# Passage between two stages, end of the kernel and a wait of GpSimd laid out anew

## The chip, the cores and the metric

One core of a Trainium2 chip runs the kernel. Its engines are TensorE (PE), VectorE (DVE), ScalarE (ACT), GpSimd (POOL) and SyncE (SP, which only issues transfers here); each runs its own queue of instructions in order, and they meet at semaphores. The metric is device time in microseconds of one launch, the median of the runs.

## The reference

A cross attention and a gated feed-forward layer, each added to its input, over x of 128 x 64 x 128 (batch, sequence, channels) in fp32, with 16 heads of 8 channels:

```python
x = x + attention(layernorm(x), ctx, ctx)      # per batch 64 x 64 scores, 16 heads
z = layernorm(x)                               # 8192 rows of 128
def gate(z, conv_w, conv_b, gamma, beta, lin_w, lin_b):
    xc = einsum('ngf,gf->ng', z.reshape(n, 32, 4), conv_w) + conv_b
    xn = batchnorm(xc)                         # mean and variance over ALL 8192 rows
    return softmax(gelu(xn) @ lin_w.T + lin_b) # 128 logits per row
so, si = gate(z, so_...), gate(z, si_...)      # keep the 32 largest of 128 in each row
out_branch = (z @ W) * top32(so)
in_branch  = (z * top32(si)) @ W
x = x + out_branch + in_branch + bias
```

The batch norm needs every row before the first gate can be computed. That splits the kernel in two.

## The kernel before

The 128 batches are worked on in 16 groups of 8 (4 "pairs" of 128 rows, 512 tokens). **The first stage** is a software pipeline over steps t = -3 to 18. For a group: ACT normalises x, TensorE projects queries and keys, both are split into three bf16 parts (`split_keys`, L897, and `split_queries`, L910, on POOL; DVE does the queries of groups 0 and 1), SP writes the parts to DRAM and reads them back stacked (`write_parts` L247, `stack` L261), so that a single bf16 product has nearly fp32 accuracy. `query_side` (L348) computes the scores by row, DVE takes their maxima (`row_max` L733) and parts them into two bf16 numbers (`max_parts` L741: a CAST at L744, a subtraction at L746), TensorE turns these, ACT copies them (`max_out` L578) and sends them into the stack; `key_side` computes the scores by column with the maximum already subtracted, ACT takes the exponential, `values` multiplies, `normalise` and `residual` finish x. Then DVE takes row statistics (`stats` L722), POOL works out the scale and shift of the layer norm (`rstd` L878: add, pow, product, product), ACT normalises (L550), TensorE turns and convolves (`turn_x2`, `convolve`), ACT stores the 64 gate channels of the group (L631) and DVE takes their statistics (L802).

On POOL the order of a step t is: `rstd(t+3)` of the attention's norm, `split_keys(t+2)`, `split_queries(t+2)`, `rstd(t-2)` of the second norm, `add_bias(t+1)`. On SP: loads of ctx (t+3) and x (t+5), stack of keys and then of queries of group t+1 (12 transfers), writes of the parts of group t+2.

**The passage**: when group 15's gate channels are in, DVE aggregates (L840), POOL makes the batch norm's scale and shift in five small instructions (L941 to L949), ACT, which meanwhile has renormalised groups 0 and 1 (`again`, L648: 8 activations), loads the Gelu table with an activation on nothing (L659) and applies Gelu to all 16 groups (L664).

**The second stage** runs over 16 groups. TensorE computes the logits (`logits` L491). DVE finds the 32 largest of each of 8 blocks of 128 x 128 (4 pairs, 2 gates) in four rounds of MAX8 (L859) and MATCH_REPLACE8 (L868); once in a group it takes the reciprocal of the sums of exponentials (L873), in the last round for group 0, and one round earlier for the others. ACT takes the exponentials of the logits (L692) and later of what the rounds have left (L676); POOL subtracts them (L963, both gates in one instruction), multiplies the inner gate onto the normalised x (L967) and assembles the output (L971 to L979); TensorE turns (L529) and multiplies by W (L534), ACT scales (L705); SP stores (L292).

## Time and profile before

| | |
|---|---|
| median of 3 runs | 564.16 us (558.95 to 564.75) |
| the profiled execution | 563.33 us, of which span 560.8 us |
| DVE busy | 440.5 us (79% of the span) |
| PE busy | 405.9 us (72%) |
| ACT busy | 375.1 us (67%) |
| POOL busy | 330.2 us (59%) |
| first stage (up to the last transfer of a stack) | 0 to about 265 us |
| tail of it and passage | 265 to 309 us |
| second stage | 309 to 546.6 us |
| end | 546.6 to 560.8 us |

The profile is of one execution. Its span goes from the first to the last instruction; 2.5 us of the 563.33 lie around it. A row of the time line has start, duration, engine, line, operation, what is written and read, how many instructions are merged, and in brackets how long the engine stood idle before and what released it. SPq and ACTq are queues' issues of transfers. Shares of busy time are a mean over stages that have different limits, so the rows below are from single stretches.

### The profile page before, as it was taken

How to read it: one execution, taken by the hardware profiler on the slowest of the kernel's cores; microseconds unless marked ns; L12 is line 12 of the kernel's file. 1: busy time of each engine (PE TensorE's matmuls, PEld its weight loads, DVE VectorE, ACT ScalarE, POOL GpSimd, SP SyncE). 2: the span in 40 equal slices, each digit the busy share in tenths (PEclk: the TensorE clock that was granted, in tenths of full speed). 3: DMA queues.
4: the chain of work that ended last, by engine and by line, in shares of the span. 5: the costliest groups of instructions: out<-in, count | busy, mean ns of one | idle time of the engine just before them, and what ended most of it. 6: DMA issues, size and time to landing. Idle time of an engine off the chain costs nothing.

```text
span 560.8 us, 15570 instructions
## 1 busy us (share of the span) xinstructions
PE 405.9 (72%) x5186; PEld 316.1 (56%) x5186; DVE 440.5 (79%) x2165; ACT 375.1 (67%) x1060; POOL 330.2 (59%) x402
## 2 busy tenths in 40 slices
PE   3467988999998999988992766666666666666432
PEld 1135766777777777777860545545555555445331
DVE  7745666777877777776541799999999999999990
ACT  2425676877788777766655967777677666676652
POOL 6466676887677777562112046666666666666666
PEclk9857999999999999999795555555555555555555
DMA  4888786888887887675000000000000000000000
GB/s 135 177 206 207 193 199 151 194 185 185 192 195 191 206 187 185 161 168 123 4 4 1 0 2 19 19 20 20 19 20 19 20 20 19 20 20 19 19 20 19
DMA packets 138680, 52.78 MB, mean 94 GB/s; under 512 B 105115, under 2 KB 130908, under 8 KB 137052
## 3 DMA queue, kind: packets, MB, share of 16 engines
q1 hardware_dynamic: 136424, 51.27, 37.8%
q8 instruction: 41, 0.67, 0.5%
q10 hardware_dynamic: 2176, 0.52, 0.4%
q14 instruction: 39, 0.31, 0.2%
HBM read 34.47 MB, written 16.78 MB: 91 GB/s over the span
## 4 chain that ended last, share of the span: by engine, by line
DVE 41%; SPq 33%; DMA 9%; PE 7%; issue 5%; POOL 2%; ACT 2%; POOLq 0%; ACTq 0%; DVEq 0%
SPq L273 30%; DVE kst L868 22%; DVE top_next L859 12%; DMA k_scratch<-k_parts 6%; DVE top_first L859 4%; DMA qst<-q_scratch 3%; SPq L258 3%; PE ps_pv L329 1%; PE ps_col L314 1%; POOL kst L963 1%; ACT x2n L550 1%; PE ps_mix L534 1%; PE ps_row L358 1%; PE ps_row L503 1%; SPq L220 1%
## 5 line engine op out<-in xcount | busy, mean ns | idle before, releaser
L738 DVE TENSOR_REDUCE m<-ps_row 128x8 f32<-128x512 f32 x128 | 82.4, 686 | 54.5 <-PE ps_row L358 54.2
L868 DVE MATCH_REPLACE8 kst<-top_next,kst 128x128 f32<-128x128 f32 x384 | 101.2, 282 | 0.0
L545 ACT ACTIVATE pT<-ps_col 128x512 f32<-128x512 f32 x128 | 68.7, 589 | 37.1 <-PE ps_col L314 37.1
L859 DVE MAX8 top_next<-kst 128x8 f32<-128x128 f32 x384 | 78.2, 282 | 0.0
L329 PE MATMUL ps_pv<-vx,pT 128*64 128x18 f32 x2048 | 72.5, 213 | 0.0
L329 PEld LDWEIGHTS ps_pv<-vx,pT 128*64 128x64 f32 x2048 | 66.1, 139 | 6.3 <-issue 4.2
L519 PE MATMUL ps_proj<-wf_sb,x2T 128*128 128x128 f32 x128 | 33.2, 441 | 45.8 <-ACT x2T L682 45.8
L519 PEld LDWEIGHTS ps_proj<-wf_sb,x2T 128*128 128x128 f32 x128 | 28.5, 328 | 52.2 <-ACT x2T L682 52.2
L550 ACT ACTIVATE x2n<-xr,nm,rs 128x128 f32<-128x128 f32 x128 | 52.6, 493 | 4.2 <-POOL nm L888 4.2
L959 POOL TENSOR_SCALAR neg_max<-top_first 128x4 f32<-128x4 f32 x32 | 7.1, 222 | 74.8 <-DVE top_first L859 74.8
L358 PE MATMUL ps_row<-kst,qst 96*64 96x128 bf16 x1024 | 42.3, 226 | 12.1 <-DMA qst<-q_scratch 12.0
L314 PEld LDWEIGHTS ps_col<-qst,kst 100*128 100x128 bf16 x1024 | 34.5, 99 | 19.7 <-issue 11.7
L314 PE MATMUL ps_col<-qst,kst 100*128 100x64 bf16 x1024 | 42.2, 196 | 3.4 <-DMA qst<-mT 3.4
L676 ACT ACTIVATE kst<-kst,neg_max 128x128 f32<-128x128 f32 x128 | 39.1, 392 | 6.5 <-DVE kst L868 6.5
L358 PEld LDWEIGHTS ps_row<-kst,qst 96*64 96x64 bf16 x1024 | 32.9, 114 | 16.5 <-DMA qst<-q_scratch 14.9
L529 PE MATMUL ps_pv<-idf,kst 128*128 128x128 f32 x64 | 17.9, 435 | 33.0 <-POOL kst L967 33.0
L963 POOL TENSOR_TENSOR kst<-kst 128x1024 f32<-128x1024 f32 x16 | 37.7, 2357 | 6.8 <-ACT kst L676 6.8
L705 ACT ACTIVATE k<-ps_mix,rsum 128x128 f32<-128x128 f32 x64 | 18.3, 368 | 34.6 <-PE ps_mix L534 34.6
L534 PE MATMUL ps_mix<-wf_sb,q 128*128 128x128 f32 x128 | 33.2, 441 | 11.0 <-ACT q L701 11.0
L534 PEld LDWEIGHTS ps_mix<-wf_sb,q 128*128 128x128 f32 x128 | 28.5, 327 | 17.4 <-ACT q L701 17.4
L881 POOL TENSOR_SCALAR ve<-ag 128x4 f32<-128x4 f32 x32 | 7.3, 227 | 52.1 <-DVE ag L730 50.3
L884 POOL TENSOR_TENSOR rs<-ve,half_neg 128x4 f32<-128x4 f32 x32 | 33.2, 1039 | 4.6
(103 smaller groups left out, 1092.7 us busy)
## 6 DMA issues: line engine op xcount, KB each, us to landing
k_scratch<-k_parts SPq DMA_DIRECT2D x32, 192.0 KB, 3.1
q_scratch<-q_parts SPq DMA_DIRECT2D x32, 192.0 KB, 3.0
kst<-k_scratch SPq DMA_DIRECT2D x32, 192.0 KB
qst<-q_scratch SPq DMA_DIRECT2D x32, 192.0 KB
xr<-in_x_dram SPq DMA_DIRECT2D x16, 256.0 KB, 4.3
cT<-in_ctxT_dram SPq DMA_DIRECT2D x16, 256.0 KB, 3.7
kst<-k_scratch SPq DMA_DIRECT2D x32, 128.0 KB
qst<-q_scratch SPq DMA_DIRECT2D x32, 128.0 KB
```

The source lines that it names most:

```text
L273: sp.dma_start(dst, src).then_inc(moved[d], 16)
L314: mm = pe.matmul(ps_col[pp][:, hh, :], k_cols(s, KROWS, h, p), qst[s][0:KROWS, h, p * SEQ:(p + 1) * SEQ], start=True, stop=True)
L329: mm = pe.matmul(pv_flat[pp * SEQ:(pp + 1) * SEQ, h * 2 * VW:(h + 1) * 2 * VW], pT[:, 2 * j + pp, hh, :], vx[s][:, 2 * hp + pp, h, :], sta ...
L358: mm = pe.matmul(ps_row[b % 2][pp * SEQ:(pp + 1) * SEQ, hh, :, :], qst[s][0:MROWS, h, p * SEQ:(p + 1) * SEQ], k_cols(s, MROWS, h, p), star ...
L519: mm = pe.matmul(ps_proj[:, p * DIM:(p + 1) * DIM], x2T[:, p * 128:(p + 1) * 128], wf_sb[:, :], start=True, stop=True)
L534: mm = pe.matmul(ps_mix[:, p * DIM:(p + 1) * DIM], xsT[:, p * 128:(p + 1) * 128], wf_sb[:, :], start=True, stop=True)
L545: act.activation(pT[:, b % PT_RING, :, :], ps_col[b % 2][:, :, :], ACT.Exp, scale=SCALE).then_inc(act_exp, 1)
L550: ins = act.activation(dst[:, p, :], xr[:, PAIRS * g + p, :], ACT.Identity, bias=nm[:, n:n + 1], scale=rs[:, n:n + 1])
L738: dve.tensor_reduce(m32[:, b // 4, :, 4 * j:4 * j + 4].rearrange("q a h -> q h a"), ps_row[b % 2][:, :, :, :], AX.X, ALU.max).then_inc(dve ...
L859: ins = dve.max(top[:, n, :], src)
L868: ins = dve.match_replace(picked[s][:, p, cols], top[:, n, :], src, PICKED)
L963: pool.tensor_tensor(expd[s][:, :, :], expd[s][:, :, :], picked[s][:, :, :], ALU.subtract).then_inc(g2_gate, 1)
```

## The change

Four places:

1. POOL waits, before `split_queries(t+2)`, until DVE has parted the first maxima of group t.
2. For the last group's second norm DVE does the add and the last product (`urgent_rstd`), and POOL only the pow. In the batch norm's coefficients likewise: POOL keeps the pow, DVE does the rest. The two calls of `again` move behind the first Gelu.
3. For the last group of the second stage: the last round of MAX8 and MATCH_REPLACE8 goes by gate (inner gates of all pairs, then outer) and not by pairs; ACT's exponentials of the rest likewise; DVE takes over the subtractions, products and sums that POOL did; POOL only adds the bias to x; TensorE turns and multiplies in halves on four banks; the scaling by the reciprocal sum and the last sum are one DVE instruction per pair, straight from PSUM; SP's last store waits for these.
4. ACT does an Identity on nothing at the very start.

```diff
--- before.py
+++ after.py
...
@@ -288,7 +290,11 @@
                     write_parts(t + 2, q_parts, q_scratch, q_out, q_moved)
 
             for g in range(GROUPS):
-                wait(sp, g2_sum, 4 * g + 4)
+                if g < GROUPS - 1:
+                    wait(sp, g2_sum, 4 * g + 4)
+                else:
+                    sp.wait_ge(d2_out, 4)
                 sp.dma_start(tile(out, g), y_sb[g % 2][:, :, :]).then_inc(out_done[g % 2], 16)
             for s in range(2):
                 sp.wait_ge(out_done[s], 16 * GROUPS // 2)
@@ -521,19 +527,36 @@
                     mm.then_inc(p2_full, 1)
                 if there(t - 1):
                     s = (t - 1) % 2
-                    wait(pe, g2_xs, t)
-                    wait(pe, a2_xsT, t - 1)
                     if t == 1:
                         pe.wait_ge(dve_attn, 2 * GROUPS)
-                    for p in range(PAIRS):
-                        mm = pe.transpose(ps_pv[:, p * 128:(p + 1) * 128], gated_x[s][:, p, :], idf[:, :])
-                    mm.then_inc(p2_xsT, 1)
-                    wait(pe, a2_xsT, t)
-                    wait(pe, a2_yin, t - 1)
-                    for p in range(PAIRS):
-                        mm = pe.matmul(ps_mix[:, p * DIM:(p + 1) * DIM], xsT[:, p * 128:(p + 1) * 128], wf_sb[:, :],
-                                       start=True, stop=True)
-                    mm.then_inc(p2_yin, 1)
+                    wait(pe, a2_xsT, t - 1)
+                    if t < GROUPS:
+                        wait(pe, g2_xs, t)
+                        for p in range(PAIRS):
+                            mm = pe.transpose(ps_pv[:, p * 128:(p + 1) * 128], gated_x[s][:, p, :], idf[:, :])
+                        mm.then_inc(p2_xsT, 1)
+                        wait(pe, a2_xsT, t)
+                        wait(pe, a2_yin, t - 1)
+                        for p in range(PAIRS):
+                            mm = pe.matmul(ps_mix[:, p * DIM:(p + 1) * DIM], xsT[:, p * 128:(p + 1) * 128], wf_sb[:, :],
+                                           start=True, stop=True)
+                        mm.then_inc(p2_yin, 1)
+                    else:
+                        pe.wait_ge(d2_last, 2)
+                        pe.wait_ge(a2_x2T, GROUPS)
+                        pe.wait_ge(a2_full, GROUPS)
+                        pe.wait_ge(a2_yin, GROUPS - 1)
+                        for half, bank in enumerate((ps_pv, ps_turn)):
+                            for p in range(2 * half, 2 * half + 2):
+                                mm = pe.transpose(bank[:, p * 128:(p + 1) * 128], gated_x[s][:, p, :], idf[:, :])
+                            mm.then_inc(p2_xsT, 1)
+                        for half, bank in enumerate((ps_mix, ps_proj)):
+                            pe.wait_ge(a2_xsT, GROUPS + half)
+                            for p in range(2 * half, 2 * half + 2):
+                                mm = pe.matmul(bank[:, p * DIM:(p + 1) * DIM], xsT[:, p * 128:(p + 1) * 128], wf_sb[:, :],
+                                               start=True, stop=True)
+                            mm.then_inc(p2_yin, 1)
...
@@ -591,6 +614,9 @@
                 act.activation(attnT[:, hp, :, :].rearrange("d p (a s) -> d a p s", a=2),
                                ps_mix[:, 0:256].rearrange("d (a p s) -> d a p s", a=2, p=2), ACT.Copy).then_inc(act_attnT, 1)
 
+            act.wait_ge(dve_half, 2)
+            act.activation(nothing[:, 1:2], nothing[:, 0:1], ACT.Identity)
             act.wait_ge(qk_in, 48)
             keys_out(0)
             for t in range(FIRST, LAST + 1):
@@ -642,6 +668,7 @@
                     attn_out(t - 1, 0)
                 if e:
                     wait(act, gp_rs2, 4 * (t - 2) + 4)
+                    wait(act, dve_nm2, 1 if t - 2 == GROUPS - 1 else 0)
                     wait(act, pe_x2T, t - 3)
                     norm(t - 2, x2n[t % 2], rs2, nm2, PAIRS * (t - 2)).then_inc(act_ln2, 1)
 
@@ -652,29 +679,42 @@
                 wait(act, g2_xs, g - 1)
                 norm(g, x2n[g % 2], rs2, nm2, PAIRS * g).then_inc(a2_x2, 1)
 
-            again(0)
-            again(1)
 
             act.wait_ge(dve_half, 2)
             act.activation(nothing[:, 1:2], nothing[:, 0:1], ACT.Gelu)
             act.wait_ge(act_conv, GROUPS)
-            act.wait_ge(gp_bn, 5)
+            act.wait_ge(dve_ab, 4)
             for g in range(GROUPS):
                 part = gates[0:2 * GATES, g * GTOK:(g + 1) * GTOK]
                 act.activation(part, part, ACT.Gelu, bias=gate_ab[:, 3:4], scale=gate_ab[:, 2:3]).then_inc(act_gelu, 1)
+                if g == 0:
+                    again(0)
+                    again(1)
 
 
             for t in range(-1, GROUPS + 1):
                 if there(t - 1):
                     s = (t - 1) % 2
-                    for p in range(PAIRS):
-                        if p % 2 == 0:
-                            wait(act, d2_rep, 8 * (t - 1) + 7 + p // 2)
-                        for gate in range(2):
-                            part = picked[s][:, p, gate * DIM:(gate + 1) * DIM]
-                            n = 2 * p + gate
-                            ins = act.activation(part, part, ACT.Exp, bias=neg_max[s][:, n:n + 1])
-                    ins.then_inc(a2_left, 1)
+                    def left(p, gate):
+                        part = picked[s][:, p, gate * DIM:(gate + 1) * DIM]
+                        n = 2 * p + gate
+                        return act.activation(part, part, ACT.Exp, bias=neg_max[s][:, n:n + 1])
+                    if t < GROUPS:
+                        for p in range(PAIRS):
+                            if p % 2 == 0:
+                                wait(act, d2_rep, 8 * (t - 1) + 7 + p // 2)
+                            for gate in range(2):
+                                ins = left(p, gate)
+                        ins.then_inc(a2_left, 1)
+                    else:
+                        for gate in (1, 0):
+                            wait(act, d2_rep, 8 * GROUPS - gate)
+                            for p in range(PAIRS):
+                                ins = left(p, gate)
+                            ins.then_inc(a2_left, 1)
...
-                if there(t - 1):
+                if there(t - 1) and t < GROUPS:
                     s = (t - 1) % 2
                     wait(act, p2_xsT, t)
                     wait(act, p2_yin, t - 1)
@@ -705,6 +745,12 @@
                         ins = act.activation(yin[:, p, :], ps_mix[:, p * DIM:(p + 1) * DIM], ACT.Copy,
                                              scale=rsum[s][:, 2 * p + 1:2 * p + 2])
                     ins.then_inc(a2_yin, 1)
+                if t == GROUPS:
+                    wait(act, p2_yin, GROUPS - 1)
+                    for half, bank in enumerate((ps_pv, ps_turn)):
+                        cols = slice(half * 256, half * 256 + 256)
+                        wait(act, p2_xsT, GROUPS + half)
+                        act.activation(xsT[:, cols], bank[:, cols], ACT.Copy).then_inc(a2_xsT, 1)
                 if t >= 1 and there(t + 1):
                     again(t + 1)
@@ -775,6 +821,13 @@
                 dve.tensor_copy(q_parts[:, 1, :], q_rest[:, :]).then_inc(dve_split, 1)
                 wait(dve, dve_split, 4 * g + 3)
                 dve.tensor_tensor(q_parts[:, 2, :], q_rest[:, :], q_parts[:, 1, :], ALU.subtract).then_inc(dve_split, 1)
+            def urgent_rstd(g, ag, ve, rs, nm, ready, added, powered, done):
+                wait(dve, ready, g + 1)
+                dve.tensor_scalar(ve[:, :], ag[:, :, 1], LN_EPS, None, ALU.add).then_inc(added, 1)
+                wait(dve, powered, 4 * g + 4)
+                dve.scalar_tensor_tensor(nm, ag[:, :, 0], -1.0, rs, ALU.mult, ALU.mult).then_inc(done, 1)
 
             def first_stats(g):
                 if there(g):
@@ -819,6 +872,9 @@
                     residual(t - 2, 1)
                     wait(dve, dve_x1, 2 * (t - 2) + 2)
                     stats(t - 2, st2, ag2, dve_st2, dve_ag2, gp_rs2, 4 * (t - 2))
+                    if t - 2 == GROUPS - 1:
+                        last = slice(TILES - PAIRS, TILES)
+                        urgent_rstd(GROUPS - 1, ag2, ve2, rs2[:, last], nm2[:, last], dve_ag2, dve_ve2, gp_rs2, dve_nm2)
...
@@ -838,6 +894,14 @@
 
             dve.wait_ge(dve_gate, GROUPS)
             dve.bn_aggr(gate_ag[:, :], gate_st[:, :, :].rearrange("c g n -> c (g n)")).then_inc(dve_gate, 1)
+            dve.wait_ge(dve_gate, GROUPS + 1)
+            dve.tensor_scalar(gate_ab[:, 0:1], gate_ag[:, 1:2], BN_EPS, None, ALU.add).then_inc(dve_ab, 1)
+            dve.wait_ge(gp_bn, 1)
+            dve.tensor_tensor(gate_ab[:, 2:3], gate_ab[:, 1:2], gcol[:, 1:2], ALU.mult).then_inc(dve_ab, 1)
+            dve.wait_ge(dve_ab, 2)
+            dve.tensor_tensor(gate_ab[:, 0:1], gate_ab[:, 2:3], gate_ag[:, 0:1], ALU.mult).then_inc(dve_ab, 1)
+            dve.wait_ge(dve_ab, 3)
+            dve.tensor_tensor(gate_ab[:, 3:4], gcol[:, 2:3], gate_ab[:, 0:1], ALU.subtract).then_inc(dve_ab, 1)
...
@@ -848,12 +912,15 @@
                 wait(dve, g2_neg, 2 * (g - 1))
                 for rnd in range(TOPK // 8):
                     top = top_first[s] if rnd == 0 else top_next
+                    by_gate = g == GROUPS - 1 and rnd == 3
+                    sets = (range(1, 8, 2), range(0, 8, 2)) if by_gate else (range(0, 4), range(4, 8))
                     for half in range(2):
                         if rnd == 0:
                             wait(dve, p2_lin, 2 * g + half + 1)
                         else:
-                            wait(dve, d2_rep, 8 * g + 2 * rnd - 1 + half)
-                        for n in range(4 * half, 4 * half + 4):
+                            wait(dve, d2_rep, 8 * g + 2 * rnd - 1 + (1 if by_gate else half))
+                        for n in sets[half]:
                             p, cols = chain(n)
                             src = ps_logits[s][half][:, p % 2, cols] if rnd == 0 else picked[s][:, p, cols]
                             ins = dve.max(top[:, n, :], src)
@@ -862,7 +929,7 @@
                         wait(dve, d2_max, 8 * g + 2 * rnd + 1 + half)
                         if rnd == 0:
                             wait(dve, g2_gate, g - 1)
-                        for n in range(4 * half, 4 * half + 4):
+                        for n in sets[half]:
                             p, cols = chain(n)
                             src = ps_logits[s][half][:, p % 2, cols] if rnd == 0 else picked[s][:, p, cols]
                             ins = dve.match_replace(picked[s][:, p, cols], top[:, n, :], src, PICKED)
...
+            s = (GROUPS - 1) % 2
+            inner, outer = slice(DIM, 2 * DIM), slice(0, DIM)
+            dve.wait_ge(a2_left, GROUPS)
+            dve.tensor_tensor(expd[s][:, :, inner], expd[s][:, :, inner], picked[s][:, :, inner], ALU.subtract).then_inc(d2_last, 1)
+            dve.wait_ge(d2_last, 1)
+            dve.wait_ge(a2_x2, GROUPS)
+            dve.tensor_tensor(gated_x[s][:, :, :], expd[s][:, :, inner], x2n[s][:, :, :], ALU.mult).then_inc(d2_last, 1)
+            dve.wait_ge(a2_left, GROUPS + 1)
+            dve.tensor_tensor(expd[s][:, :, outer], expd[s][:, :, outer], picked[s][:, :, outer], ALU.subtract).then_inc(d2_last, 1)
+            dve.wait_ge(d2_last, 3)
+            dve.wait_ge(a2_full, GROUPS)
+            dve.tensor_tensor(expd[s][:, :, outer], expd[s][:, :, outer], full_s[s][:, :, :], ALU.mult).then_inc(d2_last, 1)
+            dve.wait_ge(d2_last, 4)
+            dve.wait_ge(g2_sum, 4 * (GROUPS - 1) + 1)
+            dve.tensor_tensor(y_sb[s][:, :, :], y_sb[s][:, :, :], expd[s][:, :, outer], ALU.add).then_inc(d2_last, 1)
+            dve.wait_ge(d2_last, 5)
+            for half, bank in enumerate((ps_mix, ps_proj)):
+                dve.wait_ge(p2_yin, GROUPS + half)
+                for p in range(2 * half, 2 * half + 2):
+                    dve.scalar_tensor_tensor(y_sb[s][:, p, :], bank[:, p * DIM:(p + 1) * DIM], rsum[s][:, 2 * p + 1:2 * p + 2],
+                                             y_sb[s][:, p, :], ALU.mult, ALU.add).then_inc(d2_out, 1)
         @block.gpsimd
         def _(pool):
-            def rstd(g, ag, ve, rs, nm, ready, out_sem, used):
+            def rstd(g, ag, ve, rs, nm, ready, out_sem, used, added=None):
                 wait(pool, out_sem, 4 * g)
+                if added is not None:
+                    pool.wait_ge(added, 1)
+                    wait(pool, used, g)
+                    pool.tensor_tensor(rs, ve[:, :], half_neg[:, :], ALU.pow).then_inc(out_sem, 4)
+                    return
                 wait(pool, ready, g + 1)
                 pool.tensor_scalar(ve[:, :], ag[:, :, 1], LN_EPS, None, ALU.add).then_inc(out_sem, 1)
                 wait(pool, used, g)
@@ -929,24 +1025,19 @@
                 elif t > FIRST + 1 and there(t + 2):
                     split_keys(t + 2)
                 if t >= 0 and there(t + 2):
+                    wait(pool, dve_m, 2 * t + 1)
                     split_queries(t + 2)
                 if there(t - 2):
                     part = slice(PAIRS * (t - 2), PAIRS * (t - 1))
-                    rstd(t - 2, ag2, ve2, rs2[:, part], nm2[:, part], dve_ag2, gp_rs2, act_ln2)
+                    rstd(t - 2, ag2, ve2, rs2[:, part], nm2[:, part], dve_ag2, gp_rs2, act_ln2,
+                         dve_ve2 if t - 2 == GROUPS - 1 else None)
...
-            pool.wait_ge(dve_gate, GROUPS + 1)
-            pool.tensor_scalar(gate_ab[:, 0:1], gate_ag[:, 1:2], BN_EPS, None, ALU.add).then_inc(gp_bn, 1)
-            pool.wait_ge(gp_bn, 1)
+            pool.wait_ge(dve_ab, 1)
             pool.tensor_tensor(gate_ab[:, 1:2], gate_ab[:, 0:1], half_neg[0:2 * GATES, 0:1], ALU.pow).then_inc(gp_bn, 1)
-            pool.wait_ge(gp_bn, 2)
-            pool.tensor_tensor(gate_ab[:, 2:3], gate_ab[:, 1:2], gcol[:, 1:2], ALU.mult).then_inc(gp_bn, 1)
-            pool.wait_ge(gp_bn, 3)
-            pool.tensor_tensor(gate_ab[:, 0:1], gate_ab[:, 2:3], gate_ag[:, 0:1], ALU.mult).then_inc(gp_bn, 1)
-            pool.wait_ge(gp_bn, 4)
-            pool.tensor_tensor(gate_ab[:, 3:4], gcol[:, 2:3], gate_ab[:, 0:1], ALU.subtract).then_inc(gp_bn, 1)
...
-                if there(t - 1):
+                if t == GROUPS:
+                    g, s = t - 1, (t - 1) % 2
+                    wait(pool, out_done[s], 16 * (g // 2))
+                    pool.tensor_tensor(y_sb[s][:, :, :], tile(xr, g), bf_row[:, :].unsqueeze(1).broadcast_to([128, PAIRS, DIM]),
+                                       ALU.add).then_inc(g2_sum, 1)
+                elif there(t - 1):
...
```

## Rows read from the trace of the kernel before

**Rows 1.** Busy by stretch: length, engines' busy us (instructions), PE clock, DMA share, GB/s.

```profile
326.60:546.60 220.00, 136.26 (x464) 108.12 (x462) 219.95 (x1455) 152.09 (x574) 136.10 (x120) 0.50 0.05 19
```

**Rows 2.** Time line of SP's queue, part of one step of the first stage.

```profile
188.28 1.02 SPq L258 DMA_DIRECT2D q_scratch<-q_parts  x2
...
189.93 0.79 SPq L220 DMA_DIRECT2D xr<-in_x_dram  x1
190.87 7.12 SPq L273 DMA_DIRECT2D kst<-k_scratch  x6
```

**Rows 3.** Time line, the same step on POOL and DVE; PE at the last group.

```profile
178.96 0.61 POOL L914 CAST q_parts<-q 128x512 bf16<-128x512 f32 x1
...
181.55 1.17 POOL L920 TENSOR_TENSOR q_parts<-q_rest,q_parts 128x512 bf16<-128x512 f32 x1
...
179.68 1.15 DVE L744 CAST m_parts<-m 128x32 bf16<-128x32 f32 x1
180.87 0.65 DVE L746 TENSOR_TENSOR m_parts<-m,m_parts 128x32 bf16<-128x32 f32 x1
...
264.94 0.64 PE L358 MATMUL ps_row<-kst,qst 96*64 96x128 bf16 x16 [1.28 <-DMA qst<-q_scratch]
```

**Rows 4.** Groups by line: count, busy us and mean ns, idle before.

```profile
L744 DVE CAST m_parts<-m 128x32 bf16<-128x32 f32 x32 | 11.9, 373 | 1.1
...
L746 DVE TENSOR_TENSOR m_parts<-m,m_parts 128x32 bf16<-128x32 f32 x32 | 10.9, 341 | 1.1
```

**Rows 5.** Time line of the passage and of the second stage's group 0.

```profile
294.65 0.38 DVE L730 BATCH_NORM_AGGREGATE ag<-st 128x2 f32<-128x6 f32 x4
...
295.56 1.04 POOL L884 TENSOR_TENSOR rs<-ve,half_neg 128x4 f32<-128x4 f32 x1
...
297.23 1.65 ACT L550 ACTIVATE x2n<-xr,nm,rs 128x128 f32<-128x128 f32 x4 [2.32 <-POOL nm L888]
...
303.32 3.17 ACT L550 ACTIVATE x2n<-xr,nm,rs 128x128 f32<-128x128 f32 x8
...
304.17 0.58 DVE L840 BATCH_NORM_AGGREGATE gate_ag<-gate_st 64x2 f32<-64x96 f32 x1
...
305.14 0.57 POOL L943 TENSOR_TENSOR gate_ab<-gate_ab,half_neg 64x1 f32<-64x1 f32 x1
...
306.51 1.28 ACT L659 ACT_TABLE_LOAD   x1
...
307.92 11.38 ACT L664 ACTIVATE gates<-gates,gate_ab 64x512 f32<-64x512 f32 x16
...
319.79 1.28 ACT L692 ACT_TABLE_LOAD   x1
...
323.75 0.24 ACT L692 ACTIVATION_READ_ACCUMULATOR kst<-ps_row,neg_max 128x1 f32 x1
...
326.39 0.20 DVE L873 RECIPROCAL rsum<-sums 128x8 f32<-128x8 f32 x1
```

**Rows 6.** Time line of the end.

```profile
545.54 2.44 ACT L676 ACTIVATE kst<-kst,neg_max 128x128 f32<-128x128 f32 x8 [1.34 <-DVE kst L868]
...
551.79 1.11 PE L529 MATMUL ps_pv<-idf,kst 128*128 128x128 f32 x4 [10.41 <-POOL kst L967]
552.94 0.60 ACT L701 ACTIVATE q<-ps_pv 128x512 f32<-128x512 f32 x1 [4.96 <-PE ps_pv L529]
...
553.59 2.07 PE L534 MATMUL ps_mix<-wf_sb,q 128*128 128x128 f32 x8 [0.69 <-ACT q L701]
...
556.99 1.26 POOL L979 TENSOR_TENSOR kst<-kst,k 128x512 f32<-128x512 f32 x1 [1.34 <-ACT k L705]
```

**Rows 7.** Time line of the start: 512 columns on DVE while POOL is idle.

```profile
16.95 0.69 DVE L773 TENSOR_TENSOR q_rest<-q,q_parts 128x512 f32<-128x512 f32 x1
```

**Rows 8.** Busy by stretch of 6 us, first stage (columns as in rows 1).

```profile
92.00:98.00 6.00, 3.35 (x67) 2.40 (x67) 3.12 (x9) 2.38 (x6) 1.69 (x4) 1.00 0.81 224
...
266.00:272.00 6.00, 6.00 (x81) 5.50 (x78) 2.45 (x7) 2.89 (x6) 0.00 (x0) 0.53 0.01 3
```

2 lines of the change are left out of this document (added).

## Prediction

> **What bounds the kernel now.** I read the stretches first. The second stage, from 326.60 to 546.60, is DVE's alone: 219.95 of 220.00 us busy [rows 1]. Whatever this change gives must therefore fall ahead of that stretch or behind it, or shift its start. DVE's own order of work in the stretch isn't touched.
>
> Next the SP queue in one step of the first stage. Issues follow each other without a hole: the queries' write starts at 188.28, the load of x ends at 189.93 + 0.79 = 190.72, and the next stack starts at 190.87 [rows 2]. One step lasts as long as SP needs to issue it. TensorE runs ahead of it: at 264.94, for the last group, it had stood 1.28 us for the transfer into qst [rows 3]. So the first stage is bound by SP and its transfers, and the other engines have some slack in each step.
>
> Third, POOL and DVE in the same step. DVE's CAST of the maxima (L744) starts at 179.68 and takes 1.15 us; POOL has begun the split at 178.96 and is in it until 182.72; the subtraction behind the CAST takes 0.65 [rows 3]. Where POOL is idle the same two take 0.18 and 0.19 (the medians). Over 32 of each, the sums are 11.9 and 10.9 us [rows 4], so the stretching costs DVE 11.9 - 32 x 0.18 = 6.1 and 10.9 - 32 x 0.19 = 4.8, together 10.9 us. It is real, but in a stage that SP bounds.
>
> Last, the two places where the engines hand work to each other and nothing overlaps: the passage (rows of 294 to 327) and the end (from 545.5).
>
> **The change, part by part.** The sum is made against the profiled execution: 563.33 us, of which 560.8 are span. The median of the three runs is 564.16, 0.8 above it.
>
> *The wait ahead of the queries' split (14 times).* dve_m reaches 2t + 1 when DVE has done L746. Without the stretching that is 179.68 + 0.18 + 0.03 + 0.19 = 180.08, and POOL would start the split at about 180.2 in place of 178.96: 1.2 us late. Behind it on POOL stand rstd of group t-2 (ACT waits for it before it normalises, and TensorE for that), add_bias and the next group's rstd and keys' split, each of which may shift by the same 1.2. The split now ends at 181.55 + 1.17 = 182.72 and would end at 183.9; SP wants it at 188.28 [rows 2, 3], so 4.3 us of slack remain and SP's queue doesn't notice. DVE, no longer stretched, is 1.4 us earlier in exchange. TensorE saves about 1 us of waiting for mT's source in such a step, and spends it waiting for SP. I take 0. The bounds are a gain of 10.9 us, if all the stretching lay on the path, and a loss if something on POOL's queue came late for SP, which begins at 4.3 us more delay.
>
> *The last group's normalisation.* Now: DVE's aggregate ends at 294.65 + 0.38 = 295.03, POOL does four instructions, ACT starts at 297.23: 2.20 us. After: DVE's add (0.19, priced as L746), POOL's pow alone (1.04), DVE's nm (0.19), ACT. With the hand-overs of the rows near by (0.06, 0.12, 0.04, 0.10) that is 1.74: 0.46 us saved [rows 4, 5]. DVE stands behind that wait for 1.2 us with group 14's bn_stats queued behind it; its next use is at 303 [rows 5], so this is covered.
>
> *The coefficients of the batch norm.* Now bn_aggr ends at 304.17 + 0.58 = 304.75 and POOL does five instructions; ACT, which has been renormalising groups 0 and 1 (3.17 us from 303.32), loads Gelu's table (1.28) and starts the first Gelu at 307.92 [rows 5]. After: DVE's add 0.06 + 0.19, POOL's pow 0.09 + 0.57, DVE's three products and differences 0.04 + 3 x 0.21, hand-over to ACT 0.10, together 1.68. With the 0.46 from above the first Gelu starts at 304.75 - 0.46 + 1.68 = 305.97. ACT's table is loaded in that shade: the renormalising now begins at 303.32, so the load would start at 302.9 and end at 304.2. DVE's second stage thus begins 307.92 - 305.97 = 1.95 us earlier.
>
> *The two renormalisations moved behind the first Gelu.* They take 3.1 us on ACT (3.17 less the overlap with the neighbour), and 15 Gelus, the exp table and group 0's eight exponentials are queued behind them. Those end now at 323.75 + 0.24 = 323.99, and DVE's reciprocal in group 0's last round, which needs their sums, runs at 326.39 [rows 5]: 2.4 us of cover. After: ACT ends at 323.99 - 1.95 + 3.1 = 325.1; DVE arrives at 326.39 - 1.95 = 324.44. A new wait of 0.7 us appears there, and the reciprocal starts near 325.2. The passage as a whole gives 326.39 - 325.2 = **1.2 us**, not 1.95. The Trainium skill (ScalarE: Activation LUTs, What ACT_TABLE_LOAD costs) puts a switch of sets at 2.66 us, a drain of 1.38 included. The rows show 1.28 and no drain between ACT's last instruction and the load [rows 5]; by the page the table would be ready at 302.9 + 2.66 = 305.6, still before the coefficients, and the sum would be the same.
>
> *The end.* Now: ACT's eight exponentials start at 545.54 (2.44 us), then come POOL's difference and product, four transposes 1.11 from 551.79, a copy, four products 2.07 from 553.59, four scalings, POOL's sum 556.99 + 1.26 = 558.25, then the store [rows 6]. After, in steps: the first four exponentials (inner gates of all tiles) start at 545.54 as now, since the inner half of the replacements is as long as half 0 was; they end at 546.81 (3 x 0.29 + 0.39). DVE, idle from 546.6 on, subtracts the inner 512 columns, 546.91 to 547.60 (0.69 by L773), and multiplies to 548.39 [rows 7]. PE's first two transposes (0.66 of the four's 1.11) end at 549.11, the others at 549.56. ACT's half copy takes about 0.4 (the whole is 0.60): 549.55. PE's first two products 549.6 to 550.65, the other two to 551.66 (halves of 2.07). DVE in the shade: outer difference, product and sum, 548.42 to 550.69. Then four scalar_tensor_tensor of 128 columns from PSUM; no row shows one. 32 columns take 0.19 and 512 take 0.69 [rows 4, 7]; on the line between them 128 take 0.29, less a little for the overlap of two: 0.27. The second pair starts at 551.72 and ends at 552.25. POOL's xr + bf_row has no wait left after group 14's sum and runs before any of it. **558.25 - 552.25 = 6.0 us.** Bounds: with DVE's 512 columns at POOL's 1.16 [rows 3] the inner two cost 0.9 more and the outer three trail to 553.0, the store is issued near 554.1, a gain of 4.2; with 0.35 each (the half) the gain is 6.7.
>
> *The Identity at the start* moves the first table load ahead of the first use. ACT's first result goes to POOL, and SP was then held by DVE's fill of kst; 0, at most 0.3.
>
> **Sum.** 563.33 - 1.2 - 6.0 = 556.1.
>
> **Rivals.**
> (a) *The stretching was on the path.* Each step is shorter by what DVE regains. For it: TensorE's slack at the start of the last group is only 1.28 us, so the stage is nearly balanced. Against it: SP's queue has no hole in which to wait for anybody [rows 2]. All of it gives 556.1 - 10.9 = 545.2, half of it 550.7.
> (b) *Renormalising between Gelus reloads tables.* ACT loads Gelu's table, then Identity's, then Gelu's again: 2 x 1.28 = 2.56 more in front of group 0's exponentials, whose cover is spent. The passage would lose 1.4, and the time be 556.1 + 2.6 = 558.7. Against it: the only load behind the 16 Gelus is that at the first exponential, 319.79, with x2T's copy ahead of it [rows 5]. The Trainium skill (ScalarE: Activation LUTs, Table sets) says that identity and copy are in every set; by that rule there is no reload.
> (c) *Slower: the clock.* TensorE's regained time becomes idle time in one piece ahead of each step. After its wait of 1.28 us at 264.94 the granted clock was 0.53 over the window 266 to 272, near its lower level of 1.2 GHz [rows 3, 8]. Six us at 0.53 hold the work of 3.2 us at 1.00. If that happened in the middle of the stage, that step would need 2.8 us more on TensorE, mT would come late, and SP waits for mT before the next stack. With no slack at all the kernel is slower than before from the third fall on (7.2 / 2.8 = 2.6), and by over 1% from the fifth; with seven in 14 steps the time is 556.1 + 19.6 = 575.7. Against it: the window 92 to 98 had only 3.35 us of busy time and kept 1.00 [rows 8].
> (d) *The end is mis-sized.* DVE at its dear bound: 556.1 + 1.8 = 557.9. With another slow step of SP in the same run it is within 1%.
>
> **How the numbers follow.** The forecast has 0.70; (a) 0.08; (b) 0.08; (c) 0.06; (d) 0.08. About 1% (5.6 us of 564.16) is what a measurement of this kernel can tell from no change; the runs before lie between 558.95 and 564.75, so the time moves by about that much of itself. 1% faster is below 558.5. The forecast falls there nearly always (0.64 of 0.70), (a) always, (b) and (d) in part: faster 0.75; slower, the far half of (c) and bad luck in the first stage, 0.05; same 0.20. The range goes from half of (a), 550.7, to (b) in a run 1.3 us slow in the first stage, 560.0.
>
> **What would show it.** The first Gelu near 306.0; a wait of DVE's reciprocal for ACT in group 0 of the second stage, with the second stage otherwise the same 220 us; L744 and L746 at 0.18 and 0.19 in all or nearly all steps, with TensorE's waits for mT's source moved into waits for qst; from the last exponential to the store some 6 us less. The prediction is wrong if SP's queue shows holes ahead of the queries' write, or its steps get shorter on the mean, if a table load stands among the Gelus, or if TensorE's clock is low in steps where it was full.

## The result, and the profile after

| | before | changed | ratio |
|---|---|---|---|
| median | 561.82 us (20 runs, 556.7 to 564.75) | 553.69 us (20 runs, 548.26 to 564.89) | 0.9847 [0.9819, 0.9875] |
| the same pair again, in the experiments | 561.57 us (13 runs) | 555.87 us (8 runs) | 0.9878 [0.9831, 0.9924] |

The change makes the kernel 8.6 us faster (7.0 to 10.2) by the ratio; the forecast was 556.1 us, faster. The ratio and its interval are taken over fast executions alone, which leaves out four of the changed kernel's 20 and none of the kernel before; over all 20 of each the medians are 8.1 us apart and the means 7.1. The profiled execution of the changed kernel was one of its longest (564.89 us, span 562.6), so a second profile of the same kernel, 555.40 us with a span of 553.6, stands beside it below.

The passage first. The time line of the changed kernel, all engines, answers to [rows 5]:

```profile
304.22 0.17 DVE L828 TENSOR_SCALAR ve<-ag 128x4 f32<-128x4 f32 x1
304.63 1.04 POOL L974 TENSOR_TENSOR rs<-ve,half_neg 128x4 f32<-128x4 f32 x1 [6.86 <-DVE ve L828]
305.70 0.16 DVE L830 SCALAR_TENSOR_TENSOR nm<-ag,rs 128x4 f32<-128x4 f32 x1 [1.30 <-POOL rs L974]
...
305.94 1.65 ACT L573 ACTIVATE x2n<-xr,nm,rs 128x128 f32<-128x128 f32 x4 [1.89 <-DVE nm L830]
...
312.15 1.28 ACT L684 ACT_TABLE_LOAD   x1
...
312.88 0.58 DVE L896 BATCH_NORM_AGGREGATE gate_ag<-gate_st 64x2 f32<-64x96 f32 x1
...
313.72 0.54 POOL L1040 TENSOR_TENSOR gate_ab<-gate_ab,half_neg 64x1 f32<-64x1 f32 x1 [8.06 <-DVE gate_ab L898]
...
314.92 0.81 ACT L689 ACTIVATE gates<-gates,gate_ab 64x512 f32<-64x512 f32 x1 [1.27 <-DVE gate_ab L904]
315.64 3.17 ACT L573 ACTIVATE x2n<-xr,nm,rs 128x128 f32<-128x128 f32 x8
...
334.10 0.20 DVE L940 RECIPROCAL rsum<-sums 128x8 f32<-128x8 f32 x1 [0.60 <-ACT kst L732]
```

The row statistics of the last group end at 304.19. From there DVE's 0.17, POOL's 1.04, DVE's 0.16 and hand-overs of 0.38 together lead to ACT's normalising at 305.94. The table load (312.15 to 313.43) now lies ahead of the coefficients, and no load stands behind the first Gelu (314.92): the renormalising follows it directly, and the other fifteen Gelus follow at 318.71, the end of the renormalising being 318.81. The last row holds the new wait, 0.60 us.

The end, in the same kernel's time line, answers to [rows 6]:

```profile
553.31 2.44 ACT L702 ACTIVATE kst<-kst,neg_max 128x128 f32<-128x128 f32 x8 [1.41 <-DVE kst L935]
554.62 0.69 DVE L946 TENSOR_TENSOR kst<-kst 128x512 f32<-128x512 f32 x1 [0.30 <-ACT kst L702]
...
556.14 0.66 PE L552 MATMUL ps_pv<-idf,kst 128*128 128x128 f32 x2 [6.99 <-DVE kst L949]
...
558.35 1.06 PE L557 MATMUL ps_proj<-wf_sb,q 128*128 128x128 f32 x4
558.68 0.61 DVE L962 SCALAR_TENSOR_TENSOR kst<-ps_mix,rsum,kst 128x128 f32<-128x128 f32 x2 [0.58 <-PE ps_mix L557]
559.45 0.61 DVE L962 SCALAR_TENSOR_TENSOR kst<-ps_proj,rsum,kst 128x128 f32<-128x128 f32 x2 [0.16 <-PE ps_proj L557]
```

Before, 12.71 us passed from the start of the last exponentials (545.54) to the end of the last instruction ahead of the store (558.25) [rows 6]; now it is 560.06 - 553.31 = 6.75.

Between the two lies the second stage. Only the order of its last round is changed, for the last group, and its length isn't: from the reciprocal of group 0 to the end of the last MATCH_REPLACE8 it is 220.16 us before and 220.22 in both profiles of the changed kernel. Busy time by stretch, changed kernel (length, busy of PE, PEld, DVE, ACT, POOL, then PE clock, DMA share, GB/s), answers to [rows 1]:

```profile
334.30:554.30 220.00, 138.20 (x470) 109.95 (x468) 220.00 (x1456) 151.77 (x574) 137.20 (x121) 0.50 0.05 19
```

The first stage. Groups by line of the changed kernel (count, then busy us and mean ns, then idle time before and its releaser), answers to [rows 4]:

```profile
L790 DVE CAST m_parts<-m 128x32 bf16<-128x32 f32 x32 | 10.1, 317 | 1.1
...
L1010 POOL CAST q_parts<-q 128x512 bf16<-128x512 f32 x14 | 8.5, 610 | 24.1 <-DVE m_parts L792 24.1
...
L792 DVE TENSOR_TENSOR m_parts<-m,m_parts 128x32 bf16<-128x32 f32 x32 | 6.1, 192 | 1.1
```

The subtraction fell from 10.9 to 6.1 us, 0.19 each. The CAST only went from 11.9 to 10.1. POOL stands 24.1 us in 14 waits for it. The stage did not get shorter: the last row statistics end at 295.03 before, and at 304.19 and 295.20 in the two profiles after. The 9.0 us between these two, which are the same kernel, are the subject of the last experiments.

### The profile page after: what moved, and what is told of

The parts are those of the page before. It is cut to its first block, busy times and chain, and to the rows that moved or that the text cites. A ratio compares the mean times of both kernels' runs of the same rounds, so it can differ in the third digit from the quotient of the medians.

```text
span 562.6 us, 15584 instructions
## 1 busy us (share of the span) xinstructions
PE 422.0 (75%) x5186; PEld 329.1 (59%) x5186; DVE 439.9 (78%) x2180; ACT 375.3 (67%) x1058; POOL 321.8 (57%) x390
## 4 chain that ended last, share of the span: by engine, by line
DVE 42%; PE 27%; SPq 11%; DMA 9%; ACT 6%; issue 3%; POOL 1%; DVEq 0%; ACTq 0%; POOLq 0%
DVE kst L935 21%; DVE top_next L926 12%; SPq L275 11%; PE ps_pv L335 7%; PE ps_col L320 4%; DVE top_first L926 4%; PE ps_row L364 4%; DMA qst<-mT 4%; DMA k_scratch<-k_parts 3%; PE ps_mix L350 2%; ACT gates L689 2%; DMA qst<-q_scratch 2%; PE ps_proj L396 2%; PE ps_proj L384 2%; PE ps_proj L390 1%
## 5 line engine op out<-in xcount | busy, mean ns | idle before, releaser
L335 PE MATMUL ps_pv<-vx,pT 128*64 128x18 f32 x2048 | 77.9, 219 | 0.0
L335 PEld LDWEIGHTS ps_pv<-vx,pT 128*64 128x64 f32 x2048 | 71.4, 148 | 7.4 <-issue 5.2
L364 PE MATMUL ps_row<-kst,qst 96*64 96x128 bf16 x1024 | 44.6, 234 | 8.3 <-DMA qst<-q_scratch 8.3
L320 PEld LDWEIGHTS ps_col<-qst,kst 100*128 100x128 bf16 x1024 | 36.2, 102 | 22.6 <-issue 12.7
L320 PE MATMUL ps_col<-qst,kst 100*128 100x64 bf16 x1024 | 44.1, 200 | 5.6 <-DMA qst<-mT 5.4
L364 PEld LDWEIGHTS ps_row<-kst,qst 96*64 96x64 bf16 x1024 | 35.2, 120 | 12.2 <-DMA qst<-q_scratch 10.4
L541 PE MATMUL ps_mix<-wf_sb,q 128*128 128x128 f32 x120 | 31.1, 441 | 10.3 <-ACT q L741 10.3
L1060 POOL TENSOR_TENSOR kst<-kst 128x1024 f32<-128x1024 f32 x15 | 35.3, 2352 | 2.8 <-ACT kst L702 2.7
L935 DVE MATCH_VALUE_LOAD kst<-top_next,kst 128x8 f32 x384 | 36.8, 96 | 0.0
L541 PEld LDWEIGHTS ps_mix<-wf_sb,q 128*128 128x128 f32 x120 | 26.7, 327 | 16.3 <-ACT q L741 16.3
L980 POOL TENSOR_TENSOR rs<-ve,half_neg 128x4 f32<-128x4 f32 x31 | 32.2, 1037 | 4.5
```

The costliest lines, as they stand in the source:

```text
L320: mm = pe.matmul(ps_col[pp][:, hh, :], k_cols(s, KROWS, h, p), qst[s][0:KROWS, h, p * SEQ:(p + 1) * SEQ], start=True, stop=True)
L335: mm = pe.matmul(pv_flat[pp * SEQ:(pp + 1) * SEQ, h * 2 * VW:(h + 1) * 2 * VW], pT[:, 2 * j + pp, hh, :], vx[s][:, 2 * hp + pp, h, :], sta ...
L364: mm = pe.matmul(ps_row[b % 2][pp * SEQ:(pp + 1) * SEQ, hh, :, :], qst[s][0:MROWS, h, p * SEQ:(p + 1) * SEQ], k_cols(s, MROWS, h, p), star ...
L541: mm = pe.matmul(ps_mix[:, p * DIM:(p + 1) * DIM], xsT[:, p * 128:(p + 1) * 128], wf_sb[:, :], start=True, stop=True)
L935: ins = dve.match_replace(picked[s][:, p, cols], top[:, n, :], src, PICKED)
```

## Experiments

The theory: the time comes from the end (6.0 us) and the passage (1.2), and POOL's wait is worth nothing, since SP's queue and its transfers pace the first stage. The main rivals: the wait gives part of the time (a), and the wait costs time through idle pieces on TensorE that lower its clock (c). The unit of reading is the distance between fixed points, since the start of everything behind the first stage moves by 9.0 us between two profiles of one kernel. All ratios are to the kernel before, run beside each kernel.

### The parts, one at a time

The wait alone, put into the kernel before:

```diff
                 if t >= 0 and there(t + 2):
+                    wait(pool, dve_m, 2 * t + 1)
                     split_queries(t + 2)
```

> The kernel before with POOL's wait ahead of the queries' split alone. Theory A (the first stage is bound by SP's queue; DVE's regained time goes nowhere): the same as before within 0.3% (561.8 +- 1.5); L744 and L746 (the CAST and the subtraction of the maxima) near 0.18 and 0.19 in most steps; split later by about 1.2 us a step. Theory B (the stretching was on the path, the gain beyond 7.2 us comes from here): 1.4 us or more faster, 560.4 or less. Theory C (TensorE's idle time gathers ahead of each step and its clock falls): slower, with windows of clock 0.50 in the middle of the first stage and SP waiting for ACT's mT.

Measured: 562.78 us beside 562.08, ratio 1.0035 [0.9996, 1.0075]. That is +2.0 us, with bounds of -0.2 and +4.2: no gain, so (a) falls (its half would have been 0.990), and a small loss isn't excluded.

The passage alone (`urgent_rstd`, the coefficients of the batch norm with POOL's pow only, `again` behind the first Gelu), put into the kernel before; three pieces of the edit:

```diff
-            again(0)
-            again(1)
...
-            act.wait_ge(gp_bn, 5)
+            act.wait_ge(dve_ab, 4)
...
+                if g == 0:
+                    again(0)
+                    again(1)
```

> The kernel before with the passage alone changed (last group's norm and batch norm coefficients shared between DVE and POOL, renormalising moved behind the first Gelu). Theory A: 1.2 us faster, 560.6: from the last row statistics to the reciprocal of group 0 1.2 us shorter, with a wait of the reciprocal for ACT's exponentials of about 0.7. Rival: the reciprocal does not wait and the whole 1.95 us come through: 559.9. Rival: tables are reloaded between the Gelus: 1.4 us slower, 563.2.

Measured: 561.27 us, ratio 1.0014 [0.9976, 1.0051]. One to two us can't be told from nothing in the total; the expectation is settled by the time line. The last statistics end at 293.95, and this is DVE's row of the reciprocal:

```profile
323.88 0.20 DVE L895 RECIPROCAL rsum<-sums 128x8 f32<-128x8 f32 x1 [0.61 <-ACT kst L696]
```

It is 29.93 behind the statistics; before it was 326.39 - 295.03 = 31.36 [rows 5]. The passage gives 1.43 us, and the new wait is 0.61. The distance hardly moves of itself: in the three profiles with the old passage (before, the wait alone, the end alone) it is 31.36 to 31.38, in four with the new one (this one, both of the changed kernel, and that of the changed kernel without the wait) 29.91 to 29.93.

The end alone (all the hunks of point 3 of the change; the first is shown), put into the kernel before:

```diff
-                wait(sp, g2_sum, 4 * g + 4)
+                if g < GROUPS - 1:
+                    wait(sp, g2_sum, 4 * g + 4)
+                else:
+                    sp.wait_ge(d2_out, 4)
```

> The kernel before with the end alone changed. Theory A: 6.0 us faster, 555.8: from the start of the last exponentials to the last instruction that the store waits for 6.75 us in place of 12.71. Rival: DVE's operations at their dear bound: 4.2 us faster, 557.6.

Measured: 553.83 us, ratio 0.9890 [0.9836, 0.9944], a gain of 6.2 us (3.1 to 9.2). From the last MATCH_REPLACE8 to the end of the span it is 8.20 us, against 14.25 before: 6.05.

The changed kernel without the wait:

```diff
                 if t >= 0 and there(t + 2):
-                    wait(pool, dve_m, 2 * t + 1)
                     split_queries(t + 2)
```

> The changed kernel without POOL's wait ahead of the queries' split. Theory A: equal to the changed kernel, 7.2 us under the kernel before (ratio 0.987), since the wait is worth nothing. Theory B: about 1.4 us slower than the changed kernel would be beside it (ratio 0.987 where the changed kernel has 0.9847). Theory C: no slower, and with fewer falls of TensorE's clock in the first stage.

Measured: 553.93 us, ratio 0.9870 [0.9826, 0.9915]; with the wait 0.9847 [0.9819, 0.9875] and 0.9878 [0.9831, 0.9924]. From this side the wait is worth 1.3 us gained by the first comparison and 0.4 lost by the second. The two kernels didn't run side by side, and each of these ratios has an interval of 0.003 to 0.005 to either side, 1.6 to 2.6 us. Together with the wait alone: nothing that can be measured, of either sign.

DVE's two small instructions tell why that is no contradiction to what the wait does. L744/L746 of before, busy us by kernel (32 of each):

| kernel | CAST | subtraction | both |
|---|---|---|---|
| before | 11.9 | 10.9 | 22.8 |
| passage alone | 10.8 | 13.2 | 24.0 |
| end alone | 9.0 | 13.7 | 22.7 |
| changed, no wait | 9.8 | 12.1 | 21.9 |
| wait alone | 9.5 | 6.2 | 15.7 |
| changed | 10.1 | 6.1 | 16.2 |
| changed, second profile | 10.2 | 6.2 | 16.4 |

The wait gives DVE back some 6 to 7 us, spread over the stage, and the stage keeps its length. All of it is the subtraction's: the CAST has 9.0 to 11.9 us in the four kernels without the wait and 9.5 to 10.2 in the three profiles with it.

The chain of work that ended last tells why it goes nowhere. Over 80 to 250 us of the kernel before it reads:

```profile
by line: SPq L273 69.3%; DMA k_scratch<-k_parts 12.2%; SPq L258 7.5%; issue 4.9%; DMA qst<-q_scratch 2.3%; SPq L220 1.8%; SPq L224 1.7%; PE ps_row L358 0.8%; PE ps_col L314 0.6%; SPq L53 0.3%
```

SP's issues and the transfers they wait for are nearly all of it, TensorE has 1.4%, DVE nothing. Whether an issue of SP is as long as it is by itself, or because the DMA engines are busy (a mean share of 0.78 over this stretch), is not separated here.

### What moving the two renormalisations is worth

```diff
+            again(0)
+            again(1)
+
             act.wait_ge(dve_half, 2)
             act.activation(nothing[:, 1:2], nothing[:, 0:1], ACT.Gelu)
...
-                if g == 0:
-                    again(0)
-                    again(1)
```

> The changed kernel with the two renormalisations back in front of the Gelu table's load. Theory A (their move is worth its gain less the lost cover): the first Gelu 12.89 - 0.46 = 12.4 us after the last row statistics (10.73 in the changed kernel), the reciprocal of group 0 waits for nobody and stands 31.36 - 0.46 = 30.9 us after them (29.9 in the changed kernel), so the move brings 1.0 us. Rival (the move only shifts the wait): the reciprocal at 29.9 as well.

One run, 560.35 us (before on the same chip 563.24). ACT's load and then DVE's reciprocal in its time line (ACT renormalises from 305.83 to 309.00):

```profile
309.02 1.28 ACT L686 ACT_TABLE_LOAD   x1
```

```profile
328.90 0.20 DVE L939 RECIPROCAL rsum<-sums 128x8 f32<-128x8 f32 x1
```

The statistics end at 297.98. The table is ready at 310.30, later than the coefficients, and becomes the bound: the reciprocal comes 30.92 behind the statistics, without a wait, against 29.93 with the move. So the move is worth 1.0 of the 1.43 us, and the shorter chains alone only 0.44. The total of one run says nothing here; the time behind the statistics does.

Then one step further, so that the wait of 0.6 goes too. Group 1's renormalisation moves behind group 0's exponentials:

```diff
                 if g == 0:
                     again(0)
-                    again(1)
...
-                if t >= 1 and there(t + 1):
+                if t >= 0 and there(t + 1):
                     again(t + 1)
```

> The changed kernel with the second renormalisation moved behind group 0's exponentials, where ACT waits for DVE. Theory A (DVE's new wait of 0.6 us is ACT's queue): the reciprocal of group 0 waits for nobody, 29.3 us after the last row statistics in place of 29.9. Rival (something else holds it): 29.9.

One run, 555.55 us. The statistics end at 296.07. Rows of ACT, and of DVE, from its time line:

```profile
307.52 1.63 ACT L573 ACTIVATE x2n<-xr,nm,rs 128x128 f32<-128x128 f32 x4
```

```profile
325.29 0.21 DVE L939 RECIPROCAL rsum<-sums 128x8 f32<-128x8 f32 x1
```

29.22 behind the statistics and no wait: another 0.7 us of the passage.

### How much delay the wait may cause

The prediction's bound spoke of a delay beyond SP's slack of 4.3 us. Here POOL waits for the second parted maxima of the group in place of the first, some 7 us later:

```diff
-                    wait(pool, dve_m, 2 * t + 1)
+                    wait(pool, dve_m, 2 * t + 2)
```

> The changed kernel with POOL's wait one count later, so that the queries' split waits for the second half of the maxima, some 8 us after the first. Theory A (the wait is free because SP has about 4 us of slack behind the split): now SP's write of the queries' parts waits for POOL in every step, 3.5 us or more each, 40 us or more slower in 14 steps. Rival (SP's queue has no say and the slack is larger): within 1% of the changed kernel.

Measured: 666.4 us, ratio 1.1868. SP's waits in this kernel (total us, times, longest):

```profile
SPq L53 <- POOL q_parts L1016: 98.3, 14, 10.3
```

Its time line on SP, and on POOL, in one step (the split ends at 208.23 + 1.15 = 209.38):

```profile
202.53 0.92 SPq L260 DMA_DIRECT2D k_scratch<-k_parts  x2
209.45 0.89 SPq L260 DMA_DIRECT2D q_scratch<-q_parts  x2
```

```profile
205.63 0.61 POOL L1010 CAST q_parts<-q 128x512 bf16<-128x512 f32 x1 [10.24 <-DVE m_parts L792]
```

SP has written the keys by 203.45 and stands until the split ends at 209.38. So SP does wait in every step, as theory A says. But it isn't SP's wait that sets the length. The kernel is 110.5 us slower than the changed kernel beside it (105 than the kernel before), and the mean SP step from group 3 to group 15 is 24.4 us in place of 15.4. The chain of work that ended last, over one step:

```profile
185.10 1.15 POOL q_parts L1016
...
186.70 1.05 POOL rs L980
...
188.78 1.25 ACT x2n L573 x3
...
203.56 0.25 PE ps_row L364 x8
...
208.23 1.15 POOL q_parts L1016
```

No issue of SP and no transfer stands in it. The wait closes a ring through POOL's own queue: behind the split stands the second norm's `rstd`, ACT waits for that before it normalises and takes its next exponentials (0.49 us of pT behind x2n in the chain), TensorE waits for these, the scores for the last maxima of a group come at the end of TensorE's order of work, and the next split waits for those maxima. One turn takes 208.23 - 185.10 = 23.1 us. The CAST, now never beside a POOL instruction, takes 0.182 in the mean over all 32, so the unstretched price in the prediction was right, and it is of no use.

### Where the runs of one kernel differ

The two profiles of the changed kernel differ by 9.0 us at the last statistics, and not behind them. Busy PE and its granted clock by stretch in the longer one (columns: length, PE busy, clock, DMA share, GB/s):

```profile
50.00:56.00 6.00, 6.00 (x80) 0.50 0.85 213
...
62.00:68.00 6.00, 6.00 (x88) 0.50 0.90 251
...
146.00:152.00 6.00, 3.20 (x64) 0.83 0.91 261
152.00:158.00 6.00, 6.00 (x62) 0.50 0.86 154
...
262.00:268.00 6.00, 6.00 (x81) 0.50 0.78 125
```

And its SP waits, then its SP queue (kst is the stack of the keys, qst that of the queries, mT the turned maxima that ACT sends into it):

```profile
SPq L275 <- ACT mT L605: 13.1, 5, 5.2
```

```profile
65.38 0.95 SPq L222 DMA_DIRECT2D xr<-in_x_dram  x1
...
71.60 6.55 SPq L275 DMA_DIRECT2D kst<-k_scratch  x6
```

TensorE is busy without a hole at the lower of its two levels (0.50, 1.2 GHz) from 50 to 68, mT comes late, and SP stands 5.2 us before group 3's stack: the mechanism of rival (c). But it needs no wait of POOL: with the end alone the stack starts at 71.68 (SP's longest wait for mT is 5.8), with the wait alone at 71.56, in the second profile of the changed kernel at 71.45, with `again` first at 71.40; and before at 65.69, with the passage alone at 65.78, without the wait on POOL at 66.08. (With `again(1)` later, and with products only at t = 15 below, the fall is shorter and the stack starts at 67.8 and 67.7.) So the late start stands in four of six profiles with the wait and in one of four without. That the wait makes the fall likelier is neither shown nor excluded by so few. The mean SP step from group 3 to group 15 is 15.35 us with the wait alone, 15.4 in the second profile of the changed kernel, 15.55 before, 15.45, 15.0 and 15.2 in the three others without the wait, and 15.8 in the long profile.

Both profiles of the changed kernel have this first fall, so it isn't what sets them 9.0 us apart. The long one has two more. At 146 to 164 its clock is low (0.83, 0.50, 0.53 in the three stretches; 1.00 in all three of the second profile), SP waits 5.1 us for mT, and the step from one stack to the next lasts 170.76 - 151.18 = 19.6 us, against 163.82 - 149.57 = 14.3. And at 260 to 272 the clock is low again, and from SP's last issue to the last statistics it is 33.06 us, against 29.37. At SP's last issue the long profile is 5.3 us behind the other, and another 3.7 come behind it. In the long profile's chain over 80 to 250 us TensorE has about 80 of 170 us and SP's queue 44, where the second profile has 1 and 135: in this long execution TensorE sets the pace for much of the stretch, in this short one SP's queue.

Before, the stretches of PE at the first fall read:

```profile
44.00:50.00 6.00, 3.91 (x35) 0.54 0.79 240
...
56.00:62.00 6.00, 5.65 (x140) 1.00 0.73 174
```

The clock had fallen there too, at 44 to 50, and was back at 56. The changed kernel without the wait (3.50 us of work at 44 to 50) was back at 56 as well, the second profile of the changed kernel (3.48) wasn't. The work ahead of the fall doesn't tell them apart.

To test the clock as the cause, TensorE gets work that nobody reads (eight fp32 products of 128 columns into a bank that the scores overwrite), before the scores of every group from 1 on:

```diff
+            def fill(g, n):
+                wait(pe, dve_max, 8 * g - 1)
+                for _ in range(n):
+                    pe.matmul(ps_row[0][:, 0, :, :], wk_sb[:, :], wq_sb[:, :], start=True, stop=True)
...
+                if c and t >= 1:
+                    fill(t, 8)
                 if c:
                     query_side(t, 0)
```

> The changed kernel with eight fp32 products of 128 columns (about 1.1 us at full clock, results overwritten) on TensorE ahead of each step's first row scores from t = 1 on, where it otherwise stands idle for the transfer into qst. Theory A (the first stage's run-to-run excess is TensorE's clock falling after idle time, SP then waiting for ACT's mT): fewer windows of clock 0.50 between 60 and 270 us, no SP wait for mT there, the stretch from SP's last qst issue to the last row statistics 29.6 in place of 33.1 us; 3 to 8 us faster than the changed kernel. Rival (the falls come whatever TensorE does, or the products cost more than they give): same or up to 1.1 us a step slower.

Measured: 569.97 us, ratio 1.0148 [1.0085, 1.0210]. A miss, and the work was mis-sized. PE in its time line:

```profile
167.09 2.05 PE L371 MATMUL ps_row<-wq_sb,wk_sb 128*128 128x128 f32 x16
```

The eight products took 2.05 us at the full clock, not 1.1, and each shows as two instructions. The end of the kernel before had the price already: four of them in 2.07 us [rows 6], at a clock of 0.50. SP now waits for mT in 13 steps (20.6 us together), and a step takes 16.7 us. The step without them is 15.0 to 15.55, so of the 2.05 some 1.2 to 1.7 lengthened it. By that estimate TensorE's slack in a step is 0.3 to 0.9 us. From 68 to 300 the clock was full in every stretch of 6 us of this profile, and over the whole execution it is 0.757 to 0.777 in the six executions of this kernel, against 0.723 to 0.763 in the eleven of the kernel before beside it. So what TensorE does in the idle places does bear on the clock, but the filling cost more than it saved.

Only before the last group (t = 15), where SP has nothing more to be held up with:

> As the kernel with products in every step, but only ahead of the last group's (t = 15). Theory A (the fall at 264 to 272 us comes from the idle time in front of the last group): the stretch from SP's last qst issue to the last row statistics 29.6 in place of 33.1 us, 3.5 us faster than the changed kernel. Rival (the fall comes anyway, the products only add): 33.1 or more, 0 to 1 us slower.

The edit is that of the kernel above with `if t == GROUPS - 1` in place of `if c and t >= 1`. Measured: 554.81 us, ratio 0.9857 [0.9801, 0.9913]. Its clock at 266 to 272, PE alone (262 to 268 and 272 to 278 read 1.00 too):

```profile
266.00:272.00 6.00, 6.00 (x127) 1.00 0.01 3
```

The fall that before had at this place (0.53) [rows 8] is gone. From SP's last issue to the last statistics it is 30.55 us, against 33.04 before and 33.06 in the long profile after. But the second profile of the changed kernel has 29.37 and the wait alone 29.58 without any filling, as the fall isn't in every execution; the seven other profiles without filling, all with a fall between 248 and 278, have 32.2 to 33.7. In the time the filling doesn't show.

At the first fall, eight products at t = 1 ahead of `key_side(0, 0, 0)`:

> The changed kernel with eight fp32 products on TensorE ahead of group 0's first column scores (t = 1), where it waits for the transfer of mT near 44 to 46 us. Theory A (the run-to-run steps of some 5.8 us come from a fall of TensorE's clock behind this idle time): no low clock from 50 to 70 us, SP's stack of group 3 starts near 66 in place of 71.5 us, median 2 to 3 us under the changed kernel. Rival (the fall has another cause): the clock low there as often as before, same time.

Measured: 556.84 us, ratio 0.9876 [0.9814, 0.9937]. Its clock, in a profile of its longest execution (560.53 us):

```profile
56.00:62.00 6.00, 5.71 (x141) 1.00 0.77 144
62.00:68.00 6.00, 4.27 (x69) 0.89 0.84 227
68.00:74.00 6.00, 6.00 (x74) 0.50 0.71 146
...
144.00:150.00 6.00, 4.07 (x36) 0.60 0.87 238
```

The fall at 50 to 62 is gone and group 3's stack starts at 66.97, but falls now come from 68 on and at 144 to 150. The kernel of the next experiment, with the same eight products, has its stack at 66.01 and falls at the same two places (0.50 over 68 to 74, 0.57 over 146 to 152). Filling one idle place took away one fall, and others came later.

All that had looked useful at once: `again(1)` later, eight products at t = 1, four at t = 15:

> The changed kernel with the second renormalisation behind group 0's exponentials (0.7 us), eight products at t = 1 and four ahead of the last group. Theory A: 0.7 + 2.5 from the first fall and 2 from the one at the last group, about 5 us under the changed kernel, ratio to the kernel before about 0.978. Rival (falls come elsewhere instead): 0.7 us under the changed kernel.

Measured: 555.46 us, ratio 0.9891 [0.9848, 0.9933], not better than the changed kernel. Its passage is 29.23, as expected; what differs between the two is within the movement of the first stage. The changed kernel once more, beside it:

> The changed kernel once more, beside the three that go with it, and for a profile of an undisturbed run of it. Theory A: 7.4 us under the kernel before (1.45 from the passage, 5.97 from the end, as read from the profiles of the parts), ratio 0.987; from the last row statistics to the reciprocal 29.9, from the last replacement to the end of the span 8.3. Theory B (the wait of POOL brings something of its own): ratio 0.985 or less.

Measured: 555.87 us, ratio 0.9878 [0.9831, 0.9924]. PE, and DVE's reciprocal, of this second profile:

```profile
56.00:62.00 6.00, 6.00 (x84) 0.50 0.73 153
...
262.00:268.00 6.00, 4.43 (x118) 1.00 0.69 170
```

```profile
325.13 0.20 DVE L940 RECIPROCAL rsum<-sums 128x8 f32<-128x8 f32 x1 [0.62 <-ACT kst L732]
```

It has the first fall and not the last. The reciprocal comes 29.93 behind the statistics (29.91 in the first).

## Why the prediction was right, and where it was not

| step | predicted | measured |
|---|---|---|
| POOL's wait | 0 | 0 (alone +2.0, -0.2 to +4.2; within the changed kernel -1.3 and +0.4 by the two comparisons) |
| last group's norm: statistics to ACT | 1.74 | 1.75 |
| coefficients: aggregate to first Gelu | 1.68 | 1.46 |
| first Gelu earlier by | 1.95 | 2.16 |
| new wait of the reciprocal | 0.7 | 0.60 to 0.62 |
| passage, net | 1.2 | 1.43 to 1.45 |
| last exponentials to the store | 12.71 - 6.0 = 6.71 | 6.75 |
| end, net | 6.0 | 5.97 to 6.05 |
| Identity at the start | 0 | no run held it alone; ACT's first result came at 7.59 and 7.34 in place of 8.76, the first stack of keys at 22.86 and 22.63, before 22.20 |
| sum | 7.2 | 7.4, in the total 8.6 (7.0 to 10.2) |

**The total.** The forecast is 2.4 us above the median of 553.69. Of that 1.5 us is its base, an execution of 563.33 where the median before is 561.82.

**The wait.** Right in its value, as far as it was measured, and right in its reason: the theory that the stage lasts as long as SP takes to issue it held where half or all of 10.9 us of DVE's time had been claimed, and the chain of the kernel before has SP's queue and no DVE in it. The reason was incomplete. SP's queue does have holes in some executions, for mT, and TensorE's slack in a step is under 1 us (the filled kernel), so TensorE is nearly as much the bound as SP, and where its clock falls it is the bound. The prediction called this balance the evidence for (a); it is real, and yet DVE's regained time didn't show. The sign for it came out in half: between 60 and 260 us TensorE's waits for DVE's parted maxima fell from 6.0 us to 1.1 (second profile), but those for the transfer into qst didn't grow (7.9, then 6.4). Where the rest of that time went isn't shown, except that in this stretch TensorE also stood at the lower clock at 60 to 68.

**The signs of being wrong.** Two that the prediction named did show. TensorE's clock was low in a step where it had been full (56 to 68 in both profiles), and SP's queue had a hole ahead of the queries' write, once, 1.0 us, in the long one. The forecast held all the same. The fall also comes without the wait, so as signs these two couldn't tell a wrong prediction from the movement between executions.

**The sign in the profile that missed.** "L744 and L746 at 0.18 and 0.19 in all or nearly all steps" holds for the subtraction and fails for the CAST. The failed step is the one that put all stretching down to the queries' split. The rows of the second profile, DVE and then POOL, show other instructions beside the CAST:

```profile
152.94 0.48 DVE L790 CAST m_parts<-m 128x32 bf16<-128x32 f32 x1
...
160.16 0.69 DVE L790 CAST m_parts<-m 128x32 bf16<-128x32 f32 x1
```

```profile
152.22 1.16 POOL L1004 TENSOR_TENSOR k_parts<-k_rest,k_parts 128x512 bf16<-128x512 f32 x1
153.71 0.61 POOL L1010 CAST q_parts<-q 128x512 bf16<-128x512 f32 x1 [0.33 <-DVE m_parts L792]
...
159.53 1.27 POOL L990 TENSOR_TENSOR xr<-xr,bo_row 128x512 f32<-128x512 f32 x1
```

POOL is still in the keys' split until 153.38; the CAST of the first maxima ends at 153.42. The subtraction behind it is free, since POOL then stands at the new wait. The CAST of the group's second maxima stands beside POOL's bias add (L990). Before, eight of the twelve CASTs above 0.3 us stood beside the queries' split, two beside the keys' and two beside the bias add. In the second profile ten of the eleven stand beside the bias add, which the new wait moves back on POOL's queue. So the change removed the subtraction's share, 4.8 us, and nothing of the CAST's 6.1 that can be told from its movement between kernels (9.0 to 11.9 without the wait): it took one neighbour away and put another there. The Trainium skill (SBUF — State Buffer, Who interferes with whom) says that VectorE and GpSimd share a pair of ports, that a cast can use it in its two-port mode and an operation with two inputs in SBUF needs its read side, and that whoever issues first keeps the other out for the whole instruction. The rows agree, with 0.18 alone, and with 0.48 and 0.69 ending 0.04 and 0.05 us behind POOL's instruction; in which mode this CAST runs no run shows.

**The slack.** 1.2 us of delay was expected for the split and 4.3 us of slack for SP. POOL stood at the new wait for 1.0 us in the mean of 14 steps in the second profile (13.6 us) and 1.7 in the long one. There SP did wait for POOL's split once, 1.0 us, where the clock was low and POOL had stood for up to 4.6 us. The prediction's bound on the dear side named only what comes late for SP. With 7 us more of delay the path that closed was another, over `rstd` behind the split on POOL's queue and ACT to TensorE, and it cost 9 us per step. The 4.3 us of SP's slack were not tested by it.

**The passage.** The terms of the coefficients were a little dear, 0.22 us together. DVE's small instructions on 64x1 took 0.15 us each, three of them 0.52 from the first start to the last end and not 0.63, which is 0.15 of it with the add; the rest lies in the pow (0.54 for 0.57) and the hand-overs. The rest follows: the Gelu comes 0.2 earlier, the reciprocal too. The order of bounds was right: the coefficients first, then the exponentials that `again` pushes back.

**The end.** Nearly every part is within 0.1 us of the row it was priced by, DVE's 512 columns at 0.69 and the transposes at 0.66 among them. The first two products took 1.22 us for 1.05, which the second two (1.06) made up. Only the new instruction was mis-sized on the path: scalar_tensor_tensor of 128 columns takes 0.35 (0.61 for two) and was priced at 0.27 (0.53 for two), while its first input came 0.04 earlier. That the whole is off by only 0.04 is in part luck: the product with x2n ended 0.12 earlier than priced, and the longer first products and the new instruction took that back. The dear bound of each 512 columns at POOL's price was never near.

**The rivals.** (a) fell with the wait alone and with the kernel without it. (b) fell with one group of 15 Gelus and two table loads behind the first stage, as before. (d) fell with 6.75. (c) is half right: its mechanism exists and costs 5 to 6 us when it strikes at group 3, but it doesn't need the wait. What sets it off stays open. It occurs with the wait (four of six profiles) and without (one of four), differs between executions of one kernel, and comes elsewhere when an idle piece is filled. Nor is it shown that it explains all of the spread from 548 to 565 us; it covers the 5.5 us at group 3, the 5.3 of the step at 151 in the long profile, and about 3.5 us behind SP's last issue (32.2 to 33.7 against 29.4 and 29.6).

**What the total has beyond the parts.** 8.6 - 7.4 = 1.2 us lie within the interval, the second comparison gives 6.9, and the means over all 20 executions of each are 7.1 apart. No part of it is claimed for the wait.

## What to carry to other kernels

Price a serial tail instruction by instruction, from rows of the same shapes with the hand-overs between them: the end and the passage came out within 0.1 and 0.3 us that way, while the total alone couldn't have shown the passage at all. When the engine freed from a stretch is not what the stage's pacing queue waits for, the freed time goes nowhere, and a wait that buys it may only use slack that has been read off first, for everything that stands behind it in the same queue and not for the pacing queue alone (here 7 us more of delay cost 110, over a neighbour in POOL's queue). Where executions differ by more than the effect, measure distances between fixed points of the trace, and look for the point behind which they agree. Before a wait is put in to keep two engines apart, look at what else it moves: here it brought the next instruction beside the same neighbour.

## What the runs showed of the hardware

- TensorE at the lower level although it has no idle time: 6.00 of 6.00 us busy at 0.50 over three stretches in a row from 50 to 68 us, where another execution was back at the upper level from 56 on.
- A DVE instruction of 0.18 us was drawn out beside POOL to as much as 1.23 in the changed kernel (1.24 in its second profile), and ended 0.03 to 0.05 us behind POOL's instruction in all of the 21 CASTs above 0.3 us in these two profiles.
- A table load takes 1.28 us, and the Gelu could start right behind it; it was hidden wholly only once nothing stood ahead of it on ACT, which was worth 1.0 us.
- From the last instruction ahead of the store to the end of the span it was 2.54 us in the changed kernel, and 3.65 in the one with `again` first (3.3 to 3.5 in the three with products at one or two places): SP's final wait for the output transfer and what follows it differ by about 1 us between executions, which no instruction of the kernel accounts for.
